# A fused conv and attention kernel on one core: rows of a Q or K stack interleaved by block, so that each load writes partitions six apart

## The reference, cut to what matters

```
t = t + _L2_attn_ref(_ln_t(t), L2_attn_w_in, L2_attn_b_in, L2_attn_w_out, L2_attn_b_out)
t = t + _L2_ffn_ref(_ln_t(t), L2_ffn_weight)
t = t + _L3_attn_ref(_ln_t(t), L3_attn_w_q, L3_attn_w_k, L3_attn_w_v, L3_attn_w_o)
t = t + _L3_ffn_ref(_ln_t(t), L3_ffn_We, L3_ffn_be, L3_ffn_Wr, L3_ffn_br, L3_ffn_Wo, L3_ffn_bo)
...
scores = jnp.einsum('bhqd,bhkd->bhqk', q, k) / math.sqrt(dh)
```

## Time and profile before

| | us |
|---|---|
| three runs | 670.29, 667.11, 669.19 |
| their median | 669.19 |
| profiled execution, its own time | 668.89 |
| its span in the trace | 666.4 |
| PE busy in the span | 592.3 (89%) |
| DVE busy | 447.5 (67%) |
| ACT busy | 326.2 (49%) |
| POOL busy | 117.9 (18%) |

### The profile page before, as it was taken

The page is one execution under the profiler, slowest core; times in us unless marked ns, Lnnn a source line. Parts: engine busy times, 40 slices in busy tenths (PEclk is TensorE's granted clock), DMA queues, the critical chain, the costliest instruction groups (busy, mean ns, idle before and its releaser), DMA issues.

```text
span 666.4 us, 11227 instructions
## 1 busy us (share of the span) xinstructions
PE 592.3 (89%) x4159; PEld 407.4 (61%) x4206; DVE 447.5 (67%) x1275; ACT 326.2 (49%) x548; POOL 117.9 (18%) x115
## 2 busy tenths in 40 slices
PE   5884876767899999999999989999999999999897
PEld 2743434645667767777777767566675756565443
DVE  4668858727676686685785676776858667675464
ACT  2336658615666666665666554344443535353110
POOL 2021000242223233223123122011020200000000
PEclk9986898796999999999999999999999999999999
DMA  9400000499684593584483481608053170000000
GB/s 336 213 0 0 1 0 6 82 149 147 81 148 85 64 146 82 67 140 90 63 142 81 65 143 42 101 17 142 2 112 47 55 105 17 1 17 0 17 12 20
DMA packets 40253, 50.64 MB, mean 76 GB/s; under 512 B 4052, under 2 KB 33492, under 8 KB 39892
## 3 DMA queue, kind: packets, MB, share of 16 engines
q1 hardware_dynamic: 40200, 49.94, 40.3%
HBM read 35.11 MB, written 14.68 MB: 75 GB/s over the span
## 4 chain that ended last, share of the span: by engine, by line
PE 59%; DVE 15%; issue 3%; ACT 2%; DMA 2%; SPq 1%; POOL 0%; DVEq 0%; ACTq 0%
PE ps L1252 14%; PE ps L1135 8%; PE ps L1127 8%; PE ps L1209 5%; PE ps L1198 5%; DVE nmax L1419 4%; PE ps L1119 3%; PE ps L1194 3%; PE ps L1178 3%; PE ps L1170 3%; PE ps L1216 2%; DVE acc L1499 2%; PE ps L1173 2%; DVE xn L1375 2%; DVE stats L1364 2%
## 5 line engine op out<-in xcount | busy, mean ns | idle before, releaser
L1419 DVE TENSOR_REDUCE nmax<-ps 128x2 f32<-128x512 f32 (+1 forms) x192 | 130.9, 687 | 75.9 <-PE ps L1178 48.1
L1312 ACT ACTIVATE PT<-ps 128x512 f32<-128x512 f32 x192 | 113.4, 598 | 116.3 <-PE ps L1198 114.7
L1252 PE MATMUL ps<-wm,xnT 128*128 128x512 f32 x256 | 119.9, 599 | 0.7
L1079 POOL TENSOR_TENSOR rstd<-ve,fix 128x2 f32<-128x2 f32 x32 | 22.2, 695 | 323.8 <-DVE ve L1370 323.8
L1306 ACT ACTIVATE QS<-ps 8x1024 bf16<-8x1024 f32 x64 | 65.1, 1017 | 26.3 <-PE ps L1183 24.2
L1198 PE MATMUL ps<-QS,KS 110*128 110x256 bf16 (+3 forms) x512 | 74.5, 247 | 0.0
L1499 DVE SCALAR_TENSOR_TENSOR acc<-ps,gate,acc 128x256 f32<-128x256 f32 x128 | 61.6, 482 | 18.5 <-PE ps L1252 16.2
L1252 PEld LDWEIGHTS ps<-wm,xnT 128*128 128x128 f32 x256 | 45.1, 190 | 39.7 <-issue 38.1
L1127 PE MATMUL ps<-xnT,by_dim 128*128 128x256 f32 x256 | 63.9, 397 | 2.2 <-ACT xnT L1277 2.2
L1099 POOL TENSOR_TENSOR parts<-rest,fix 128x512 bf16<-128x512 f32 x30 | 38.1, 1271 | 140.3 <-DVE rest L1388 97.5
L1194 PE MATMUL ps<-fixb 128*128 128x256 bf16 (+1 forms) x192 | 59.9, 312 | 2.3 <-DVE nmax L1419 2.0
(11 more groups left out here) (211 smaller groups left out, 913.7 us busy)
## 6 DMA issues: line engine op xcount, KB each, us to landing
parts_dram<-parts SPq DMA_DIRECT2D x32, 384.0 KB, 3.3
QS<-parts_dram SPq DMA_DIRECT2D x96, 128.0 KB
KS<-parts_dram SPq DMA_DIRECT2D x96, 128.0 KB, 7.9
wt<-wt_dram SPq DMA_DIRECT2D x1, 2562.0 KB, 18.6
wm<-wm_dram SPq DMA_DIRECT2D x1, 2449.0 KB, 13.2
xc<-x_dram SPq DMA_DIRECT2D x8, 256.0 KB, 5.4
out_dram<-res SPq DMA_DIRECT2D x8, 256.0 KB, 2.1
w<-w_dram SPq DMA_DIRECT2D x1, 845.0 KB, 7.7
```

The costliest lines, as they stand in the source:

```text
L1252: mm = pe.matmul(d, normT(stage, batch)[:, c, t * P:(t + 1) * P], M("We", c * EXPERTS * CH + e * 2 * CH, 2 * CH), start=(c == 0), stop=(c ...
L1312: act.activation(PT[:, pt_slot(piece, n), :], bank(piece), ACT.Exp).then_inc(drain(piece), 1)
L1419: dve.tensor_reduce(group[:, 0, :] if part == 0 else group[:, 1, 2 * part - 2:2 * part], bank(piece).rearrange("p (j n) -> p j n", n=w_), ...
```

## The change

The destination rows of each of the six loads are taken with a step of six, where they were 16 neighbours. Row d of block c now stands in partition 6 d + c, where it stood in partition 16 c + d.

```
                     for c, r in enumerate((Q_PARTS, K_PARTS)[n]):
-                        sp.dma_start((QS, KS)[n][DH * c:DH * (c + 1), stack(stage, batch)]
+                        sp.dma_start((QS, KS)[n][c:STACK:len(Q_PARTS), stack(stage, batch)]
                                      .rearrange("d (o h) n -> d o (h n)", o=NC2),
                                      parts_dram[n, r].rearrange("(o d h) n -> d o (h n)", o=NC2, d=DH))\
                             .then_inc(sems[f"stack_loaded{n}"], 16)
```

## The result

| | before | after |
|---|---|---|
| median of 7 runs, us | 669.93 | 665.57 |
| lowest to highest, us | 667.11 to 670.52 | 663.94 to 665.76 |
| profiled execution, us | 668.89 | 665.75 |
| its span, us | 666.4 | 664.0 |

The ratio is 0.9944, with a 95% interval of 0.9920 to 0.9968: the change makes the kernel 4.4 us faster by the medians, 3.8 us by the ratio. It lies in the forecast range (659.5 to 667.0) and 2.6 us above the forecast of 663.0.

What follows compares the result with a forecast made beforehand. PE carried 59% of the last chain, but the first body's slow stack loads held up stores, ACT, DVE and PE. 668.89 - 6.1 = 662.8 us profiled, 663.0 as the median; range 659.5 to 667.0.

Steps and rivals of the forecast that it cites:

- middling rate: Rival for the stack loads: rows six apart still meet, 140 GB/s, K lands at 142.7, gain 3.6 us, 665.6; chance 0.08.
- What the loads wait for: Stack loads: 16 neighbouring partitions share 4 ports into SBUF; rows six apart reach 13, rate from 107 towards 342 GB/s.
- Where it matters: Start of the attention half, 136 to 150 us: all three waits stand there; in 15 of 16 bodies nobody waits.
- step 7: All bodies from the second on: loads end sooner, but nobody waited for them, so no gain.
- Step 1: First body's loads: SP's issue ends at 136.64 us, and the last K load lands at 139.3 to 139.9.
- a rival with a threshold of 1.07 us per issue: Slower: a step of six costs SP more per DMA; at 1.74 us each 8.1 us more, 677; chance 0.05.
- Step 2: Body 1's second store: issued at 140.2 us instead of 146.27, 6.1 us earlier, with POOL's third part the next limit.
- Steps 3 and 4: Body 1's stores: first out at 137.7, second lands at 143.5; DVE's maxima 145.9, PE's split maximum 148.4, each 6.1 us earlier.
- Step 6: PE's clock after 142 us: falls again and rises as long after dense work starts, 5.7 us; no gain or loss.

Runs made afterwards that it cites:

- e5: The kernel before with each load's rows two partitions apart, 16 rows over 32 partitions, instead of six apart: 664.99 us, ratio 0.9923 to the kernel before.
- e3: The kernel before with rows six apart for the Q loads only, K loads to neighbours as before; scores wrong, only times read: 667.13 us, one run.
- e2: The kernel before with rows six apart for the 180 later loads only, the first body's twelve loads as before: 669.60 us, ratio 1.0003.
- e1: The kernel before with rows six apart for the first body's twelve loads only, the other 180 as before: 665.65 us, ratio 0.9959.
- e4: The full change plus 21 unread products in PE's gaps from 142.6 to 148.9 us: 662.11 us, ratio 0.9901 to the kernel before.
- e7: The full change plus 32 unread products in PE gaps that both kernels share, none from 142 to 149 us: 661.09 us, ratio 0.9866 to the kernel before.
- e8: The kernel before plus the same unread products in the same shared PE gaps, loads unchanged: 666.35 us.

## Why the prediction was right, and where its size was off

- **The number.** 665.57 us lies in the range, but it is just what the *middling rate* rival gave (665.6). The time alone couldn't have told it from the forecast; the landings do, 2.6 us and 308 GB/s for a full share where that rival had 140. The forecast's own range, 661.5 to 664.5, was missed by 1.1 us. That the wide range held is in part luck: its upper end was drawn for a slower load, and what took the time up to there were falls of the clock.
- **What the loads wait for.** Right. The rate of a full DMA share went from 122 to 308 GB/s by the destination's rows alone, with source, sizes and engines unchanged; e5 and e3 bear it out. That falls in with the Trainium skill's port map (SBUF — State Buffer, Door 1), and so does e5: by that map rows two apart over 32 partitions reach 8 ports, twice those of 16 neighbours. The measured rate was 1.8 times theirs (216 against 122 GB/s). For rows six apart the map gives 13 ports for four of the blocks and 14 for two. No run here separates ports from mere distance.
- **Where it matters.** Right: e2 finds nothing in the 15 later bodies. Too simple in step 7: with the first body early, body 1's loads come late at the old rate (PE waits 1.27 us in e1). The change makes them quick as well, so it doesn't cost it.
- **Step 1, the landing of K.** 139.3 to 139.9 forecast, 140.47 measured. SP had issued the loads at 138.34 us, not at 136.64: 1.83 us more for the twelve issues and 0.15 for the zeros, less 0.28 for an earlier start. I had this cost as a rival with a threshold of 1.07 us per issue; at 0.59 it was real and small.
- **Step 2, POOL as the next limit.** Not so: POOL was done at 138.55 + 1.16 = 139.71, and K's landing, bound by SP's issue, set the second store at 140.49. The store is 5.8 us earlier, not 6.1, and 0.4 us of that isn't the loads': POOL, DVE and PE already ran 0.4 us ahead of the kernel before at 130 to 139 us.
- **Steps 3 and 4.** The first store went out at 138.46, not at 137.7, behind SP's last issue, and ACT could go on at 141.69 (141.5 forecast). The second landed in 2.73 us, not in 3.28, so ACT's K part and the maxima came 0.2 to 0.3 us sooner than forecast. At the end DVE's small cast ahead of the first split maximum took 0.87 us where it takes 0.17, and PE got the split maximum at 148.85 (148.4 forecast). The cast waited for POOL: its end, 147.63 + 0.87 = 148.50, follows that of POOL's L1103, 147.32 + 1.15 = 148.47, and the same stands in e1:

```profile
146.69 1.15 POOL L1104 TENSOR_TENSOR parts<-rest,parts 128x512 bf16<-128x512 f32 x1
...
147.42 0.45 DVE L1429 CAST nparts<-nmax 128x8 bf16<-128x8 f32 x1
```

In seven profiles (the change twice, e1, e3, e4, e5, e7) this cast starts inside POOL's piece, 0.29 to 0.84 us after its start; it then takes 0.34 to 0.89 us and ends 0.02 to 0.03 us after it each time. In the other five POOL is over when the cast comes, or within 0.04 us of it, and it takes 0.17.
- **Step 6, the clock.** This is the term that was mis-sized. It fell again, as forecast, at 145.8 us. But it was back at 152.6, 3.8 us after PE's work became dense (148.85), where before it took 5.9 (154.49 to 160.4; the prediction read 5.7). So "rises as long after the dense work starts" was wrong, and the lead grew by 1.3 us there. What the sum had not at all was the clock elsewhere: the new fall at 166 us took 1.6 us, and the one near 395 us 2.9 us. For the profiled pair the account is 6.3 us of lead at the first cast, 0.7 lost to the cast, 1.3 gained, 1.6 and 2.9 lost: 2.4 us. The forecast had 6.1 and nothing for the rest. With the shared falls out of both, the change is worth 5.3 us (e7, e8).

What brings the fall near 395 us stays open. In nine profiles without products at that place only the kernels with new rows have it, and even e2 has it, though its first body isn't early; there it costs 2.6 us. The kernel before may have it in runs that weren't profiled.

## What to carry to other kernels

When a DMA's engines are busy but carry few bytes per unit of busy share, look at the partitions it touches: 16 rows in neighbouring partitions ran at 122 GB/s for a full share, the same rows two apart at 216 and six apart at 308, near the 342 of a full-width transfer, for 0.17 us more of the issuing queue. It pays only where somebody waits for the landing, and the buffers that the transfer holds back (here the store that overwrites its source, and ACT behind that) can be worth more than the wait that the trace names. A change that moves PE's work should be followed to the end of the trace, from one recurring instruction to the next: in one profile here a fall of the clock 250 us away took 2.9 of 5.4 us. Filling PE's idle gaps in both kernels gives a second comparison with fewer falls in it.

## What was not expected of the hardware

- A step between destination partitions makes an issue on SP longer, 592 ns against 424, for a step of two as for one of six. The zeros' issue behind such a load, itself unchanged, takes 0.48 us where it took 0.33.
- Products that nobody reads, in PE's idle gaps, made both kernels faster: 670.42 to 666.35 us before, with 32 products, and 661.09 us with the change, a ratio of 0.9866 (0.9848 to 0.9884) to the kernel before. Sixteen of them stand ahead of the first transpose and the first Q, where the clock had been at 1.2 GHz from 119.4 to 126.2 us before and from 118.5 to 125.3 us after.
- A DVE cast of 8 elements in each partition, which takes 0.17 us, took up to 0.89 us when it started while POOL was at a 128x512 piece, and ended with that piece.
